# Last chunk of an attention and expert kernel: gate bank read by ScalarE, projection in four banks, chunk end and bias add placed elsewhere

## What is computed

```python
x = x + attn(layernorm(x))       # 16 heads of 16, rotary embedding, softmax, out @ Wo.T + bo
x = x + moe(layernorm(x))
# moe: xc = bf16(x); normed = bf16(xc * rsqrt(mean(xc^2) + eps) * norm_weight)
#      logits = normed @ gate.T + gate_b; the top 2 of 8 experts, weighted by softmax
#      g = min(p1_even, 7); lin = clip(p1_odd, -7, 7)       # p1 = normed @ w1 + b1, per expert
#      act = g * sigmoid(1.702 * g) * (lin + 1); p2 = act @ w2 + b2
#      out = xc + bf16(sum over the experts of combine * p2)
```

## Time and profile before

| | before |
|---|---|
| median of 3 runs | 1116.25 us (1115.45 to 1118.98) |
| the profiled execution | 1118.18 us |
| its span in the profile | 1116.4 us |
| TensorE matmul / VectorE / ScalarE / GpSimd busy | 84% / 69% / 67% / 38% |
| mean granted TensorE clock | 0.94 |

### The profile page before, as it was taken

The page is one execution under the profiler, slowest core; times in us unless marked ns, Lnnn a source line. Parts: engine busy times, 40 slices in busy tenths (PEclk is TensorE's granted clock), DMA queues, the critical chain, the costliest instruction groups (busy, mean ns, idle before and its releaser), DMA issues.

```text
span 1116.4 us, 16572 instructions
## 1 busy us (share of the span) xinstructions
PE 940.6 (84%) x5217; PEld 400.6 (36%) x5288; DVE 774.1 (69%) x1529; ACT 747.5 (67%) x1017; POOL 422.0 (38%) x356
## 2 busy tenths in 40 slices
PE   4629899789888997989889998889989999996564
PEld 1412222234343443334343443334433443344243
DVE  4751211488858886588858786588867886786897
ACT  2417886777668785777668785777768887881232
POOL 2423302533264424544264434543331332334252
PEclk9758999899999998999999998999999999998587
DMA  4353536244435343444534343444534453421110
GB/s 162 99 111 78 117 82 130 67 105 115 111 91 137 88 114 86 110 103 103 125 84 125 97 110 81 107 104 105 125 78 114 105 125 88 99 91 39 48 47 29
DMA packets 79988, 109.81 MB, mean 98 GB/s; under 512 B 22531, under 2 KB 56723, under 8 KB 76819
## 3 DMA queue, kind: packets, MB, share of 16 engines
q1 hardware_dynamic: 61460, 83.47, 32.1%
q10 hardware_dynamic: 18432, 25.17, 7.6%
HBM read 82.90 MB, written 25.69 MB: 97 GB/s over the span
## 4 chain that ended last, share of the span: by engine, by line
PE 54%; DVE 17%; issue 10%; ACT 7%; DMA 4%; POOL 3%; SPq 2%; ACTq 1%; another core or an unknown queue 0%; DVEq 0%; POOLq 0%
PE OP L698 15%; PE S L684 14%; PE D L670 8%; ACT probs L815 4%; PE D L574 4%; PE BB L653 3%; PE A L653 3%; PE D L596 3%; DVE th_sb L1118 2%; DMA o_scr<-O 2%; DVE acc L1113 2%; DVE l_sb L1103 2%; DVE g_sb L1101 2%; PE D L588 2%; ACT sqs L778 1%
## 5 line engine op out<-in xcount | busy, mean ns | idle before, releaser
L815 ACT ACTIVATE probs<-S 128x1024 f32<-128x1024 f32 x512 | 513.3, 1025 | 170.1 <-PE S L684 169.4
L684 PE MATMUL S<-Qs,Ks 98*128 98x512 bf16 x1024 | 302.5, 388 | 35.6 <-ACT probs L815 19.9
L698 PE MATMUL OP<-probs,V 128*17 128x512 f32 x2048 | 276.1, 612 | 3.6 <-ACT O L824 3.6
L899 POOL TENSOR_TENSOR act_lo<-act_sb,act_hi 128x512 fp32r<-128x512 f32 x128 | 171.2, 1340 | 150.4 <-ACT act_hi L804 148.2
L684 PEld LDWEIGHTS S<-Qs,Ks 98*128 98x128 bf16 x1024 | 79.0, 99 | 217.0 <-ACT probs L815 100.4
L670 PE MATMUL D<-W,act_hi 128*128 128x256 f32 x448 | 131.9, 327 | 25.6 <-issue 14.1
L1113 DVE SCALAR_TENSOR_TENSOR acc<-D,combh,acc 128x256 f32<-128x256 f32 x224 | 97.6, 476 | 79.0 <-PE D L670 78.6
L1118 DVE SCALAR_TENSOR_TENSOR th_sb<-th_sb,g_sb 128x512 f32<-128x512 f32 x128 | 121.8, 951 | 16.9 <-ACT th_sb L791 13.1
L893 POOL TENSOR_SCALAR W<-W2b 128x512 fp32r<-128x512 bf16 x64 | 43.6, 681 | 198.6 <-PE D L670 193.4
L670 PE MATMUL D<-W,act_lo 128*128 128x256 f32 x448 | 113.4, 285 | 0.0
L804 ACT CAST act_hi<-act_sb 128x512 fp32r<-128x512 f32 x128 | 78.3, 612 | 52.0 <-DVE act_sb L1123 49.3
(11 more groups left out here) (137 smaller groups left out, 1002.4 us busy)
## 6 DMA issues: line engine op xcount, KB each, us to landing
W<-in_w ACTq DMA_DIRECT2D x64, 256.0 KB, 2.8
Ks<-k_scr SPq DMA_DIRECT2D x32, 384.0 KB
W2b<-in_w ACTq DMA_DIRECT2D x64, 128.0 KB, 2.8
Ks<-k_scr SPq DMA_DIRECT2D x32, 256.0 KB
o_scr<-O SPq DMA_DIRECT2D x32, 256.0 KB, 4.3
q_scr<-parts SPq DMA_DIRECT2D x16, 384.0 KB, 3.5
k_scr<-parts SPq DMA_DIRECT2D x16, 384.0 KB, 2.5
Qs<-q_scr SPq DMA_DIRECT2D x32, 192.0 KB
```

Of the source, the lines that this page charges most:

```text
L684: last = mm(S[:, j2, C * i:C * (i + 1)], Ks[0:SROWS + MROWS, g % 2, j, P * kt:P * (kt + 1)], Qs[0:SROWS + MROWS, g % 2, j, :], start=True, ...
L698: last = mm(OP[32 * j:32 * j + VW, :], V[:, kt, HG * g + j, :], probs[:, s % 2, C * j:C * (j + 1)], start=kt == 0, stop=kt == KT - 1)
L815: nc.scalar.activation(probs[:, s % 2, 2 * C * j2:2 * C * (j2 + 1)], S[:, j2, :], ACT.Exp, scale=SCALE).then_inc(exp_done, 1)
L899: tt(act_lo[:, e % 2, it, :], act_sb[:, a % 2, :], act_hi[:, e % 2, it, :].bitcast(FP32), ALU.subtract).then_inc(lo_s, 1)
```

## The change

In the last chunk only (`alone(u)`):

- The gate's bank is read by ScalarE: `Relu(-gate + (7 - b))` gives 7 - g, then `Sigmoid(-1.702 * that + 1.702 * 7)` takes the place of `Tanh`. VectorE's line 1101 is gone; line 1118 becomes (t - 7) * sigmoid, which is minus the wanted product, and `combh` takes the factor -1. Two constants are made at the start. `hi` of a half expert now comes after the next half expert's Relu and Sigmoid in ScalarE's order.
- The projection uses the four banks of `S` for its four token tiles. The half that belongs to the first eight heads (`wo_0`) is done at half-step 8, the other half in `wo` 0 and 1, with no wait between them.

In all chunks: `final` comes four half-steps later (after `nf`), and `x1_b` is at half-step 9 instead of 11 (before GpSimd's multiply at step 5).

```diff
-          "guard": 4, "flag": 6, "x1_in": 0, "x1_b": 11, "wo0": 13, ...
+          "guard": 4, "flag": 6, "x1_in": 0, "wo_0": 8, "x1_b": 9, "wo0": 13, ...
     h = FFN0 + ((NF + LAG - 1) * 3 // 2 * 2 if PAIRED else 3 * (NF + LAG - 1)) + 1
+    h += 4
     FINAL = h // 2
...
+        def wo_bank(u, a, bank):
+            if alone(u):
+                return S[:, a, :].rearrange("p (t c) -> p t c", t=2)[:, :, 0:E]
+            return bank[:, :].rearrange("p (t c) -> p t c", t=2)
...
-                if st in FILLS and filling[1] and (st != "guard" or n == NCH - 1):
+                if st in FILLS and filling[1] and (st != "guard" or n == NCH - 1) and not (st == "wo" and alone(u)):
                     pe.wait_ge(*read_of(*filling[1]))
...
+                elif st == "wo_0" and alone(u):
+                    pe.wait_ge(exp_done, PAIRS * B * NCH)
+                    pe.wait_ge(on_s, 2 * u + 1)
+                    project_out(0, u, (0,), None)
+                    project_out(1, u, (0,), None)
                 elif st == "wo":
                     pe.wait_ge(on_s, 2 * (u + 1))
+                    project_out(a, u, (1,) if alone(u) else range(CT), bank).then_inc(d_full, 1)
...
-                elif st == ("hidden" if alone(u) else "hi"):
+                elif st == "hi":
                     upper_half(a, u)
+                elif st == "up" and alone(u):
+                    e, it = divmod(a, 2)
+                    act.wait_ge(m1_mm, 2 * (NF * u + a) + 1)
+                    act.wait_ge(act_s, NF * u + a - 1)
+                    nc.scalar.activation(g_sb[:, a % 2, :], expert_banks(u, a)[0], ACT.Relu, bias=b1r[:, e, it:it + 1],
+                                         scale=-1.0).then_inc(g_s, 1)
+                    act.wait_ge(g_s, NF * u + a + 1)
+                    nc.scalar.activation(th_sb[:, a % 2, :], g_sb[:, a % 2, :], ACT.Sigmoid, bias=top_arg[:, 0:1],
+                                         scale=-ALPHA).then_inc(th_s, 1)
...
+                    v.tensor_scalar(b1r[:, :, :], b1_sb[:, :, 0, :], -1.0, LIMIT, ALU.mult, ALU.add).then_inc(c_set2, 1)
+                    v.memset(top_arg[:, :], ALPHA * LIMIT).then_inc(c_set2, 1)
...
+                    if not alone(u):
+                        dve.wait_ge(m1_mm, 2 * n + 1)
+                        v.tensor_scalar(g_sb[:, q, :], gate, b1f[:, e, 0, it:it + 1], LIMIT, ALU.add, ALU.min).then_inc(g_s, 1)
...
+                    if alone(u):
+                        v.scalar_tensor_tensor(th_sb[:, q, :], g_sb[:, q, :], LIMIT, th_sb[:, q, :], ALU.subtract, ALU.mult).then_inc(t1_s, 1)
```

More of the change, by code:

```diff
@@ L74, in block_kernel @@
         place(PREP, h + AT["length"] + AT[st], (st, 0))
-    for st in ("x1_in", "x1_b", "stats2", "rstd2", "xc", "ss", "ms", "rrms", "nf", "nfT", "logits", "gates1", "etop",
+    for st in ("x1_in", "wo_0", "x1_b", "stats2", "rstd2", "xc", "ss", "ms", "rrms", "nf", "nfT", "logits", "gates1", "etop",
                "gates2", "combT"):
@@ L630, in stage, with project_out @@
                     expert_down(a, u)
+            def project_out(a, u, parts_in, bank):
+                for t in range(2):
+                    tok = P * (2 * a + t)
+                    for c in parts_in:
+                        last = mm(wo_bank(u, a, bank)[:, t, :], Op[:, c, tok:tok + P], wo_sb[:, c, :],
+                                  start=c == 0, stop=c == CT - 1)
+                return last
             def expert_up(f, u):
@@ L784, in stage @@
                     nc.scalar.activation(etop[:, :], dtop[:, :], ACT.Exp).then_inc(etop_s, 1)
-                elif st == ("hidden" if alone(u) else "hi"):
+                elif st == "hi":
                     upper_half(a, u)
-                elif st == "tanh":
[L788 to L791, removed]
+                elif st == "up" and alone(u):
[7 more added lines that the diff above has]
+                                         scale=-ALPHA).then_inc(th_s, 1)
+                elif st == "tanh":
+                    if not alone(u):
+                        act.wait_ge(g_s, NF * u + a + 1)
+                        if looped(u) or u or a >= 2:
+                            act.wait_ge(act_s, NF * u + a - 1)
+                        nc.scalar.activation(th_sb[:, a % 2, :], g_sb[:, a % 2, :], ACT.Tanh, scale=ALPHA / 2).then_inc(th_s, 1)
                     e, it = divmod(a, 2)
@@ L1002, in stage @@
                     dve.wait_ge(d_full, k + 1)
-                    xh = X1s[:, n, 2 * a:2 * a + 2, :].rearrange("p t c -> p (t c)")
-                    v.tensor_tensor(xh, bank[:, :], xh, ALU.add).then_inc(x1_s, 1)
+                    xh = X1s[:, n, 2 * a:2 * a + 2, :]
+                    v.tensor_tensor(xh, wo_bank(u, a, bank), xh, ALU.add).then_inc(x1_s, 1)
                 elif st == "stats2":
@@ L1096, in expert @@
                 if st == "up":
-                    dve.wait_ge(m1_mm, 2 * n + 1)
                     if looped(u) or u or f >= 2:
                         dve.wait_ge(act_s, n - 1)
-                    v.tensor_scalar(g_sb[:, q, :], gate, b1f[:, e, 0, it:it + 1], LIMIT, ALU.add, ALU.min).then_inc(g_s, 1)
+                    if not alone(u):
+                        dve.wait_ge(m1_mm, 2 * n + 1)
+                        v.tensor_scalar(g_sb[:, q, :], gate, b1f[:, e, 0, it:it + 1], LIMIT, ALU.add, ALU.min).then_inc(g_s, 1)
                     dve.wait_ge(m1_mm, 2 * n + 2)
@@ L1117, in expert @@
                     dve.wait_ge(th_s, n + 1)
-                    v.scalar_tensor_tensor(th_sb[:, q, :], th_sb[:, q, :], 1.0, g_sb[:, q, :], ALU.add, ALU.mult).then_inc(t1_s, 1)
+                    if alone(u):
+                        v.scalar_tensor_tensor(th_sb[:, q, :], g_sb[:, q, :], LIMIT, th_sb[:, q, :], ALU.subtract, ALU.mult).then_inc(t1_s, 1)
+                    else:
+                        v.scalar_tensor_tensor(th_sb[:, q, :], th_sb[:, q, :], 1.0, g_sb[:, q, :], ALU.add, ALU.mult).then_inc(t1_s, 1)
                     dve.wait_ge(t1_s, n + 1)
```

12 lines of the change are left out of this document (4 added, 8 removed), and 2 rows, old and new, of the table AT.

## The result

The changed kernel takes 1122.49 us (median), the kernel before, measured beside it, 1115.45 us: a ratio of 1.0061, with a 95% interval of 1.0043 to 1.0079. The forecast was 1108.8 us and the range ended at 1113.0. The profiled execution of the changed kernel took 1123.97 us (span 1122.2), that of before 1118.18 us (span 1116.4).

A forecast was written before the change was run, and what follows sets the result against it. TensorE was taken to bound attention, VectorE the last chunk's experts, with an engine-to-engine chain between. Terms -4.6 - 1.15 - 0.84 + 0.1 - 1.0 = -7.5 us from the 1116.25 us median gave 1108.8 us, range 1099.0 to 1113.0.

The forecast's parts named there:

- Attention stretches, -1.0 us: Chunk 6's projection add no longer waits for the bias add, -1.0 us once; moved `final` and new holds cost zero.
- Slower: Rival: early bias add holds VectorE in attention stretches, TensorE waits in seven chunks, 11.8 us, net +4.3, 1120.6 us; chance 0.05.
- Projection, -4.6: Last chunk's projection: half the instructions move ahead, no read between parts, so its second add ends 4.6 us earlier.
- The clock at the projection: Last projection: low clock assumed; rival that it stays up gives 1.8 us more, -9.3 in all, 1107.0 us; chance 0.22.
- Norms and `final`, -1.15: Last chunk's norms: `nf` ahead of chunk 6's `final` waits for `rrms` alone, meets a W2 conversion; logits read 1.15 us earlier.
- Experts, -0.84: Last chunk's experts: line 1118 held until `lo` ends, round 3.36 instead of 3.43 us, 0.07 in twelve halves, -0.84 us.
- no hold: Rival, last chunk's experts: line 1101's time is gained whole, 9.7 us more, 1099.1 us; chance 0.12.
- experts get worse: Rival, last chunk's experts: `lo` on each round's path, rounds lose 0.7 us more, +4.2 to +8.4, 1113.0 to 1117.2 us; chance 0.15.
- Table load, +0.1: Last chunk's first Sigmoid: a second table load of 1.28 us, mostly covered by VectorE's work, costing 0.1 us.

The follow-up runs named there:

- e2: Kernel before with only the bias add moved from half-step 11 to 9 in all chunks: 1126.11 us, ratio 1.0136.
- e8: e2 with the bias add cut into four GpSimd instructions of a quarter each: 1112.78 us, ratio 0.9988 to the kernel before.
- e1: Kernel before with only `final` four half-steps later in every chunk: 1118.76 us, ratio 1.0039.
- e9: The whole changed kernel with the bias add cut into four quarters: 1108.74 us, ratio 0.9948 to the kernel before.
- e10: e4 with the bias add at half-step 9 in every chunk and cut into quarters: 1103.79 us, ratio 0.9911 to the kernel before.
- e6: Kernel before with only the last chunk's gate Relu and Sigmoid moved to ScalarE: 1114.39 us, ratio 0.9994.
- e12: Kernel before with only `final` six half-steps later, behind the shuffle: 1122.64 us, ratio 1.0079.
- e3: Changed kernel with `final` and the bias add at their old places, only the last chunk's edits left: 1111.38 us, ratio 0.9976 to the kernel before.
- e5: e4 with the bias add at half-step 9 in the last chunk only: 1110.24 us, ratio 0.9951 to the kernel before.
- e4: e3 with `final` four half-steps later in chunk 6 alone: 1108.06 us, ratio 0.9944 to the kernel before.
- e7: e4 with `lo` made of 128 of 512 tokens in the last chunk, part of the computation left out: 1100.99 us, ratio 0.9869 to the kernel before.

## Why the prediction was wrong, point by point

**Attention stretches, -1.0 us: this step failed, by some 13 us.** From the first eviction to the last it was +11.7. It had three parts.
- The failing sentence is "The bias add can also hold VectorE from a new place: it already cost one `th_sb` 1.68 - 0.68 = 1.0 us with no TensorE wait behind it. Zero." `e2` and `e8` put 12.4 us on it as medians, and a hold on the path was in the profile of before: the rows at 814.59 to 818.78. I had looked at chunks 2, 6 and 7, and taken the one that was harmless for all. The harmless and the harmful case differ in two things: in how long the instruction is held (1.0 and 2.04 us), and in what lies behind it on VectorE's queue. At 440.53 it was nothing that TensorE needed soon; at the new place it is the copy of `xnT`. In `e8` the same copy lies behind a hold of 0.41 us, and TensorE does not wait for it. The rival "Slower" had this mechanism. Its price, 1.68 us in each of seven chunks, 11.8 us, is near the 9.4 and 12.2 us of the table and the 12.4 of the medians, but that is luck: 1.68 us is the whole length of the held instruction and not its delay, and the wait for the copy that the profile shows is 4.9 us in four chunks. Its chance of 0.05 was too low.
- "`final` changes places with `nf` and `part3` on VectorE, whose sum of work [...] stays the same: zero." The sum of work did stay, but the partner on GpSimd changed: beside `rot` the pair of adds takes 2.37 us. The sum also ended at the wrong place: I counted to the next stage that TensorE needs, and left out the shuffle, which goes through GpSimd and ScalarE before TensorE needs it. Measured +3.2 us (`e1`, chunk 6's gain among it) and +5.0 us (`e9` against `e10`, the other chunks alone).
- The 0.97 us wait in chunk 6 did go: the longest wait of this kind is 0.4 us in the changed kernel. I had missed a further gain of the earlier place, at chunk end 0 (2.2 us).

**Projection, -4.6: the path was right, the size too large.** From the multiply's end it is 5.49 us instead of the 4.71 that I had summed. The projection starts 1.44 us behind the multiply, not 0.15, since chunk 6's downs, late from the hold at 1026.67, run until then; and its eight instructions take 3.25 us, not 3.76. Of the profiled 5.2 us gain (26.71 us from the last eviction to the adds' end before, 21.53 after), 1.3 is luck: the transfer for the multiply lets it start 14.77 us after the last eviction, before 16.12, and over all profiled executions of the study 14.7 to 16.1. The starting figure was a long one as well. `e1`, `e6` and `e12` have the projection of before, but in their profiles the second half took 1.99 us and not 3.78, at the high clock, and from the multiply's end to the adds' end it was 7.41 to 7.91 us, not 9.33. Against those the 5.49 is a gain of about 2 us. `e3` against `e6`, which differ in the projection alone, gives 3.9 us by the medians and 2.0 by the ratios.

**The clock at the projection: the low level, mostly.** The earlier trace rows showed 1.00 falling to 0.55. After, the stretches read 1.00, 0.96 and 0.50: `wo_0` and chunk 6's downs stand before it, but TensorE does nothing from 1030 to 1032. In `e5` the eight instructions took 1.89 us, at the high level, though TensorE stood as long before the downs (3.17 us, 3.18 in the changed kernel); what parts the two is open. In `e10` they took 1.99 us, and from the multiply's end to the adds' end it is 2.85, the 2.9 that the prediction gave for this case. So the rival was a real one.

**Norms and `final`, -1.15: right, a little low.** `nf` starts 1.12 us after `ms` ends and meets the W2 conversion, as forecast: four in 2.02 us, where four took 1.66. From the adds' end to the logits' start it is 11.95 us, before 13.45: -1.5. All nine profiles with chunk 6's `final` behind `nf` have 11.95 to 11.97 here, and all five without it 13.45 or 13.46, so this gain is sure. `e4` against `e3` gives -3.3 us between medians, with overlapping intervals.

**Experts, -0.84: the mechanism right, the gain not told from none.** The round was forecast at 3.36 us. Where GpSimd converts no `W2` it is 3.34 or 3.35, before 3.43; the last thirteen rounds took 44.60 us, 3.43 each, where it was 3.56. Relu took 0.69 us and Sigmoid 0.72, as costed. But `hi` behind the next Relu and Sigmoid, which I had put at zero, did cost: in the first round of every kernel with the edit `hi` waits behind them until TensorE has filled the gate's bank, and that round takes 4.46 to 4.48 us instead of 3.63. The last chunk's fifteen rounds take 52.4 us in all, in the kernel before 53.8, but in `e1` and `e12`, which read the gate as before, 52.9 and 52.6. `e6` shows that the edit alone brings nothing measurable, and `e7` that the hold takes the rest. The rivals "no hold" and "experts get worse" are out. The Trainium skill (page "ScalarE: Activation LUTs", section "Rules for kernel authors") gives its factor of about 3 for bf16 only, so the prediction set an fp32 tile against a figure that was not meant for it; what decides here is Relu's 0.69 us against VectorE's 0.74.

**Table load, +0.1: it cost about 0.5.** One load, 1.28 us, once. VectorE was through with the gates at 1054.88 and the first line 1150 started at 1055.40, after a wait of 0.52. The Trainium skill (page "ScalarE: Activation LUTs", section "What ACT_TABLE_LOAD costs") adds a drain of 1.38 us to each switch. The trace does not show it here: the load starts 0.02 us after Relu ends, and Sigmoid starts at 1054.65, 0.02 us after the load ends.

## What to carry to other kernels

A long GpSimd instruction that reads SBUF held VectorE's instructions with two SBUF inputs until it had ended, so its place in the order must be judged by what it holds, how long, and what stands behind the held instruction in VectorE's queue, in every chunk and not in a sample of them. Cut into shorter instructions it costs GpSimd more (3.70 us instead of 2.81) and, at the early place, the kernel less. A step that is moved for the sake of one chunk should be moved in that chunk alone: `e10` moves `final` in chunk 6 only and is 5.0 us faster than `e9`, which moves it everywhere. The bias add is the other case: once it is short, the early place serves all chunks.

## What the runs showed of the hardware that was not expected

- A held instruction is not through when its holder is: `act_sb` starts at 437.63, GpSimd ends at 439.81, `act_sb` at 440.36, 0.55 us behind; in the experts it was 0.54.
- Holding goes both ways: the bias add took 2.42 us on average in the kernel before (eight of them), and 2.70 in `e2` and in the changed kernel, where most start beside a VectorE instruction that is already running (2.81 us at 437.00, behind a `th_sb` that runs until 437.60; 2.36 at 1026.61, where it comes first).
- A late engine can move the half-clock stretches of TensorE: at 492 to 502 us the granted clock is 0.83 in `e1` and 1.00 in the kernel before, with a busy share that differs by 0.37 us of 10. Why the clock falls there is left open; from 100 to 1000 us its mean is 0.98 in both.
